# Two half sums for every f32 tile of a fused GNN stage, and a loop over two spans at once

## The reference

```python
for l in range(3):                     # gated network
    m = x @ weight[l]
    agg = segment_sum(m[src] * edge_weight[:, None], dst)
    gi, gh = agg @ w_ih.T + b_ih, x @ w_hh.T + b_hh
    r, zg = sigmoid(i_r + h_r), sigmoid(i_z + h_z)
    x = (1 - zg) * tanh(i_n + r * h_n) + zg * x
...
for W, b in ((W0, b0), (W1, b1), (W2, b2)):
    x = relu((x + segment_sum(x[src], dst)) @ W.T + b)
out = layernorm(x0 + ...)              # after each network
```

## Time and profile before

| What | Value |
|---|---|
| Median of 3 runs | 3116.35 us (3116.19 to 3117.13) |
| Profiled execution, its own time | 3116.43 us |
| Its span, first to last instruction | 3114.7 us |
[...]
| TensorE, VectorE, ScalarE busy | 3055.5 us, 1107.2 us, 909.9 us |
| Packets of TensorE's instruction fetches (q8) | 60, of 16 KB |

### The profile page before, as it was taken

The page is one execution under the profiler, slowest core; times in us unless marked ns, Lnnn a source line. Parts: engine busy times, 40 slices in busy tenths (PEclk is TensorE's granted clock), DMA queues, the critical chain, the costliest instruction groups (busy, mean ns, idle before and its releaser), DMA issues.

```text
span 3114.7 us, 74296 instructions
## 1 busy us (share of the span) xinstructions
PE 3055.5 (98%) x29956; PEld 1975.7 (63%) x29956; DVE 1107.2 (36%) x3061; ACT 909.9 (29%) x2123; POOL 291.1 (9%) x500
## 2 busy tenths in 40 slices
PE   5999999999999999999999999999999999999998
PEld 4788888888888865555555555555555555555554
DVE  5788888888888600000001010111130010001111
ACT  5666666666666510000001010011130010001111
POOL 3222222222222200000000000000000000000000
PEclk9999999999999999999999999999999999999999
DMA  5565555555555587677676777676658777786884
GB/s 183 211 248 246 224 224 246 246 234 224 237 247 240 224 331 273 264 287 279 265 274 251 280 282 282 262 269 272 258 201 332 294 288 280 298 304 260 306 310 164
DMA packets 135446, 809.63 MB, mean 260 GB/s; under 512 B 7972, under 2 KB 17432, under 8 KB 120776
## 3 DMA queue, kind: packets, MB, share of 16 engines
q1 hardware_dynamic: 129704, 800.52, 65.5%
q0 software_dynamic: 4368, 7.97, 0.9%
q10 hardware_dynamic: 1296, 0.01, 0.0%
HBM read 566.04 MB, written 242.44 MB: 260 GB/s over the span
## 4 chain that ended last, share of the span: by engine, by line
PE 98%; issue 1%; DMA 0%; DVE 0%; ACT 0%; POOL 0%; DVEq 0%; POOLq 0%; ACTq 0%
PE ps L758 33%; PE ps L924 25%; PE ps L1003 19%; PE ps L996 11%; PE ps L768 1%; PE ps L769 1%; PE ps L1029 1%; PE ps L746 1%; PE ps L1030 1%; PE ps L771 1%; PE ps L770 1%; PE ps L903 1%; PE ps L1075 0%; PE ps L892 0%; PE ps L1031 0%
## 5 line engine op out<-in xcount | busy, mean ns | idle before, releaser
L758 PE MATMUL ps<-ring,Y 128*128 128x448 f32 x2744 | 1035.7, 539 | 0.0
L758 PEld LDWEIGHTS ps<-ring,Y 128*128 128x128 f32 x2744 | 521.1, 190 | 508.8 <-issue 508.8
L924 PE MATMUL ps<-ring,Y 128*128 128x448 f16 x4116 | 780.6, 352 | 0.0
L1364 ACT ACTIVATE ring<-ps 128x392 f16<-128x392 f32 (+1 forms) x1568 | 654.1, 505 | 303.0 <-PE ps L996 298.0
L924 PEld LDWEIGHTS ps<-ring,Y 128*128 128x128 f16 x4116 | 402.7, 98 | 373.8
L1003 PE MATMUL ps<-ring,Y 128*128 (+1 forms) x2720 | 610.3, 367 | 0.4 <-ACT shared L1326 0.4
L1003 PEld LDWEIGHTS ps<-ring,Y 128*128 128x128 f32 x2720 | 487.1, 190 | 15.5 <-ACT shared L1326 0.8
L996 PEld LDWEIGHTS ps<-shared 64*128 64x128 bf16 x18816 | 337.3, 94 | 129.2 <-ACT ring L1364 82.1
L996 PE MATMUL ps<-shared 64*128 64x49 bf16 (+1 forms) x18816 | 386.7, 190 | 19.3 <-issue 16.3
L1717 DVE TENSOR_TENSOR shared<-shared 128x400 bf16<-128x400 bf16 x1176 | 396.4, 391 | 0.0
L1433 DVE SCALAR_TENSOR_TENSOR shared<-ps,bhh,shared 128x448 f32<-128x448 f32 x28 | 19.1, 684 | 775.4 <-ACT shared L1151 775.4
(11 more groups left out here) (151 smaller groups left out, 1234.7 us busy)
## 6 DMA issues: line engine op xcount, KB each, us to landing
ring<-adj_w SPq DMA_DIRECT2D x84, 2688.0 KB, 8.9
adj_w<-ring SPq DMA_DIRECT2D x56, 2744.0 KB, 12.2
ring<-adj_h SPq DMA_DIRECT2D x42, 2800.0 KB, 9.4
ring<-adj_h SPq DMA_DIRECT2D x42, 2688.0 KB, 9.1
ring<-adj_w SPq DMA_DIRECT2D x28, 2912.0 KB, 9.5
adj_h<-ring SPq DMA_DIRECT2D x56, 1372.0 KB, 5.0
x_keep<-xT SPq DMA_DIRECT2D x1, 3136.0 KB, 10.7
shared<-x_keep SPq DMA_DIRECT2D x1, 3136.0 KB, 15.4
```

The lines of the kernel that those rows point to most:

```text
L758: mm = pe.matmul(ps[:, bank, 0:GW], Y[:, h, :], ring[:, s, :, h - h0, :], start=(h == 0), stop=(last and h == TILES - 1))
L924: mm = pe.matmul(ps[:, par, 0:GW], part[:, h, :], ring_h[:, par, s, :, h - h0, :], start=(h == 0 and part is Y_high), stop=(h == TILES - 1 ...
L1364: act.activation(strip[:, :, c0:c0 + UNIT * WIN].rearrange("p h (d j) -> p d h j", d=WIN), psum_unit(a)[:, :, kind, :, :].rearrange("p d j ...
```

## The change

All 49 f32 tiles of every span are added in halves: rows 0 to 63 into bank 4 and rows 64 to 127 into bank 5. ScalarE copies both sums into two buffers. The gates take both: r, z and the input part of n each become a sum over two terms for the aggregate, so nine matmuls instead of six, of which the first two need only `x` and stand ahead of the wait for the sums. The banks of the coverage check, transpositions and gates move (transpositions now share bank 7 with the gates' n part, and wait for VectorE to have read it). In the tail the gates of span 26 come ahead of the first 13 tiles, and VectorE's addition of the two sums is gone. In TensorE's list the inner loop over slots is written out, so the body of the loop holds two spans and the slot is a constant.

```diff
-        AGG_BANK, COLUMN_BANK, RZ_BANK, IH_BANK = 4, 5, 6, 7
-        HALF_BANK = 0
-        agg_span = aggS[0][:, 0:SPAN]
+        RZ_BANK, IH_BANK, COLUMN_BANK = 6, 7, 7
+        AGG_BANKS = 4, 5
+        ROW_HALVES = [slice(r * P // 2, (r + 1) * P // 2) for r in range(2)]
+        first_banks = 5, 6
+        agg_spans = [a[:, 0:SPAN] for a in aggS]
...
                 for h in range(lo, hi):
-                    mm = pe.matmul(ps[:, AGG_BANK, 0:SPAN], Y[:, h, :],
-                                   strip_w[:, bass.ds(slot, 1), :, h, :].rearrange("p o b c -> p (o b) c"),
-                                   start=(h == 0), stop=(h == TILES - 1))
+                    for rows, bank in zip(ROW_HALVES, AGG_BANKS):
+                        mm = pe.matmul(ps[:, bank, 0:SPAN], Y[rows, h, :], strip_w[rows, slot, :, h, :],
+                                       start=(h == 0), stop=(h == TILES - 1))
...
-                pe.wait_ge(s_fev, START + n + 1)
-                if isinstance(n, int) and n == GATHERS - 1:
-                    pe.wait_ge(s_half, 1)
                 pe.wait_ge(s_frz, START + 2 * n)
                 pe.wait_ge(s_fgv, START + GV * n)
-                for c in range(2):
-                    half = ps[:, RZ_BANK, c * SPAN:(c + 1) * SPAN]
-                    pe.matmul(half, wT[:, c, :], agg_span, start=True, stop=False)
-                    pe.matmul(half, wT[:, 3 + c, :], xg, start=False, stop=True)
-                pe.matmul(ps[:, IH_BANK, 0:SPAN], wT[:, 2, :], agg_span, start=True, stop=True)
-                pe.matmul(ps[:, IH_BANK, SPAN:2 * SPAN], wT[:, 5, :], xg, start=True, stop=True).then_inc(s_fgate, 1)
+                r_z = [ps[:, RZ_BANK, c * SPAN:(c + 1) * SPAN] for c in range(2)]
+                pe.matmul(ps[:, IH_BANK, SPAN:2 * SPAN], wT[:, 5, :], xg, start=True, stop=True)
+                pe.matmul(r_z[0], wT[:, 3, :], xg, start=True, stop=False)
+                pe.wait_ge(s_fev, START + 2 * (n + 1))
+                for a in agg_spans:
+                    pe.matmul(r_z[0], wT[:, 0, :], a, start=False, stop=(a is agg_spans[1]))
+                pe.matmul(r_z[1], wT[:, 4, :], xg, start=True, stop=False)
+                for a in agg_spans:
+                    pe.matmul(r_z[1], wT[:, 1, :], a, start=False, stop=(a is agg_spans[1]))
+                for a in agg_spans:
+                    mm = pe.matmul(ps[:, IH_BANK, 0:SPAN], wT[:, 2, :], a, start=(a is agg_spans[0]),
+                                   stop=(a is agg_spans[1]))
+                mm.then_inc(s_fgate, 1)
...
                     if k == TRANSPOSE_AT:
+                        if n_gates is not None:
+                            pe.wait_ge(s_fgv, START + GV * n_gates + 2)
                         slots_to_partitions(t + 1)
...
                     if k == FIRST_BATCH:
-                        pe.wait_ge(s_fev, t)
+                        pe.wait_ge(s_fev, START + 2 * (t - 1))
...
             with pe.Fori(0, GATHERS // 2 - 1) as i:
-                with pe.Fori(0, 2) as slot:
+                for slot in range(2):
                     build_span(2 * i + slot + 2, slot, 2 * i + slot)
 
-            pe.wait_ge(s_fev, GATHERS)
+            pe.wait_ge(s_cola, GATHERS + 1)
+            fused_gates(GATHERS - 2)
             pe.wait_ge(s_bev, EV * UNITS * (1 + BATCHES * GATHERS))
             add_tiles(0, 0, SH)
-            fused_gates(GATHERS - 2)
-            pe.wait_ge(s_cola, GATHERS + 1)
             pe.wait_ge(s_found, 1)
+            pe.wait_ge(s_fgv, START + GV * (GATHERS - 2) + 2)
             pe.matmul(ps[0:1, COLUMN_BANK, 0:1], covered[:, :], ones[:, :], start=True, stop=True).then_inc(s_cov, 1)
-            add_tiles(0, SH, WHOLE_ROWS)
-            add_halves(0, WHOLE_ROWS, TILES)
+            add_tiles(0, SH, TILES)
...
-                act.activation(by_unit(agg_span), natural(ps[:, AGG_BANK, 0:SPAN]), ACT.Copy).then_inc(s_fev, 1)
+                for agg_span, bank in zip(agg_spans, AGG_BANKS):
+                    act.activation(by_unit(agg_span), natural(ps[:, bank, 0:SPAN]), ACT.Copy).then_inc(s_fev, 1)
...
-            dve.wait_ge(s_fev, START + GATHERS)
-            dve.tensor_tensor(by_unit(agg_span), by_unit(agg_span), natural(ps[:, HALF_BANK, 0:SPAN]), ALU.add)\
-               .then_inc(s_half, 1)
```

More of the change, by code:

```diff
@@ L40 @@
 SH = 13
-WHOLE_ROWS = 37
 HALF_TILES = [(0, 25), (25, 49)]
@@ L291, in gnn_program @@
         s_fagg = sem("s_fagg")
-        s_half = sem("s_half")
         s_fev = sem("s_fev")
@@ L1059, in _ @@
                 for k in range(n):
-                    mm = pe.transpose(ps[:, 6 + j % 2, k * P:(k + 1) * P], Y[:, c + k, :], ident[:, :])
+                    mm = pe.transpose(ps[:, first_banks[j % 2], k * P:(k + 1) * P], Y[:, c + k, :], ident[:, :])
                 mm.then_inc(s_setp, 1)
@@ L1074, in _ @@
                     for h in range(c, c + n):
-                        mm = pe.matmul(ps[:, 6 + k % 2, (h - c) * P:(h - c + 1) * P], xT[:, tile_cols(h)], gw[:, 0, :],
+                        mm = pe.matmul(ps[:, first_banks[k % 2], (h - c) * P:(h - c + 1) * P], xT[:, tile_cols(h)],
+                                       gw[:, 0, :],
                                        start=True, stop=True)
@@ L1343, in evac_span @@
                         act.wait_ge(s_yp0, k + 1)
-                        act.activation(Y[:, c:c + n, :], ps[:, 6 + k % 2, 0:n * P].rearrange("p (c f) -> p c f", f=P), ACT.Copy)\
+                        act.activation(Y[:, c:c + n, :], ps[:, first_banks[k % 2], 0:n * P].rearrange("p (c f) -> p c f", f=P), ACT.Copy)\
                            .then_inc(s_ye0, 1)
@@ L1370, in _ @@
                 act.wait_ge(s_setp, j + 1)
-                act.activation(xT[:, tile_cols(c, n)], ps[:, 6 + j % 2, 0:n * P], ACT.Copy).then_inc(s_xt, 1)
+                act.activation(xT[:, tile_cols(c, n)], ps[:, first_banks[j % 2], 0:n * P], ACT.Copy).then_inc(s_xt, 1)
             act.wait_ge(s_setp, NC + 1)
@@ L1745, in _ @@
                               mybir.AxisListType.XY, ALU.add).then_inc(s_found, 1)
+            fused_mix(GATHERS - 2)
             dve.wait_ge(s_cov, 1)
             dve.tensor_scalar(flag[:, :], ps[0:1, COLUMN_BANK, 0:1], float(N_EDGES), None, ALU.is_equal).then_inc(s_flag, 1)
-            fused_mix(GATHERS - 2)
             fused_blend(GATHERS - 2)
-            dve.wait_ge(s_fev, START + GATHERS)
-            dve.tensor_tensor(by_unit(agg_span), by_unit(agg_span), natural(ps[:, HALF_BANK, 0:SPAN]), ALU.add)\
-               .then_inc(s_half, 1)
             fused_mix(GATHERS - 1)
```

## The result

The changed kernel takes 3306.23 us (median of 4 runs, 3305.37 to 3307.55) against 3116.32 us before in the same session: 1.0609 times the time, interval 1.0591 to 1.0628, 190 us slower. The direction was forecast; the time lies above the range, whose upper end was 3257 us.

The account below looks back on a forecast made before the run. The prediction took TensorE, busy 98% of the span, as the bound. Visits -68 us and gates +32 us gave -36 us, the unrolled loop's fetching +143 us: from 3116.4 us to 3222 us, range 3078 to 3257 us.

Parts of the forecast that it names:

- The whole tiles' visits: TensorE's switches between 64-row builds and 128-row f32 tiles: halves save 0.21 us at each of 324, -68 us (0 to -100).
- The gates: Gate matmuls on TensorE: nine f32 ones instead of six, 0.38 us each, 28 times, +32 us, hidden by nothing.
- Their sum: Visits and gates together, before any cost of unrolling the loop: -36 us.
- The body fetched again in every iteration: TensorE's unrolled loop: the body outgrows the instruction store, all 14.3 blocks fetched anew each iteration, about 190 fetches in all.
- Rival A: The body of two spans stays in the store, no fetches in the loop: 3081 us (3048 to 3149); chance 0.20.
- The price of fetching: TensorE's loop: 9.2 us an iteration for blocks (7.3 to 11.2), 2.3 us a jump; together +143 us (+90 to +175).
- The jump: Jump back in TensorE's loop to code not in the store: 2.3 us each (0 to 2.9), 12 times, 28 us.
- rival D: VectorE becomes the bound if fetches are free, costing at most 1 us a span: 3108 us; counted within Rival A.
- B: The loop's code is fetched again but hidden, only the jump costing: 3109 us; chance 0.06.
- C: The switches give nothing and the store is outrun: 3291 us, or 3148 us with the body resident; chance 0.04.

Follow-up runs that it names:

- the second run: The kernel before with only TensorE's inner loop written out (whole tiles, two spans in the body): 3160.25 us against 3099.4 (1.0196).
- the wide halves: The changed kernel with one span in the body and two neighbouring tiles as one pair of 448-column halves streamed from `Y`: 3082.46 us against 3116.54 (0.989).
- the first run: The changed kernel with TensorE's loop rolled up to one span in the body, halves multiplying `Y` instead of the strips: 3390.66 us against 3099.4 (1.0939).
- The kernel without a loop: The changed kernel with all 26 spans of TensorE's loop written out, no jump left: 3219.85 us against 3099.4 (1.0381).

## Why the prediction was wrong

**The whole tiles' visits, right.** -68 us rested on 0.21 us a batch from the tail's switch of rows and from f16 beside f32. The trace has 1.60 for 1.71 and 0.78 for 0.88. It isn't the register instructions that fell away: whole tiles with the slot a constant still last 1.71 and the builds 0.89 (508.42, 509.31 and 511.02 us in the second run). Shown.

**The gates, right.** +32 us: nine matmuls at 0.38 us, no wait before the sums.

**Their sum, right to 2 us.** -36 us forecast, -34.1 us measured with the wide halves, whose visits and builds last as long as the change's.

**The body fetched again in every iteration, right.** 14.3 blocks forecast, 16 fetches in the iteration shown and 205 more in all (190 forecast). A slip in the count of fetched records (the earlier trace rows give 774 + 775 = 1549 for the first window, not 1559) changes nothing: one fetch per 240 either way. That the store keeps "one of 6.5 blocks and not one of twice the size" was a guess between rows; the runs put its end between 1725 and 1837 instructions, 6.7 to 7.2 blocks of 256. The size of a block shows best where code runs straight on: from 200 to 1000 us there is one fetch of 16 KB for every 257 instructions, 32388 for 126 fetches in the whole tiles without a loop and 34952 for 136 in the halves without one. Rival A's condition was never close: half of the new body is already too large, as the first run shows with 1830 instructions and 149 fetches.

**The price of fetching, wrong: this is the step that failed.** It was "the middle, 9.2" us an iteration for the blocks and "I take 2.3" us for the jump, together +143 us with an upper bound of +175. Measured, against the 3082 us that the change is worth without fetches: 224 us. The kernel without a loop splits them: 155 us for blocks (115 forecast, 141 the bound) and 68 us for jumps (28 forecast, 35 the bound), so each of the two terms was 40 us too small. The stalls were as many as foreseen, five over 1 us in the iteration shown (one of them put down to VectorE), but up to 6.0 us long where 3 was the most foreseen. The price of a block was read from whole tiles, in the loop's first pass, and carried over to halves as if a block cost the same whatever is in it. It doesn't: in code that runs straight on it is 0.34 us a block in whole tiles and 0.87 us in halves. A batch of halves has 128 instructions in 2.38 us and one of whole tiles 112 in 2.60 us, so TensorE reaches the end of a block in 4.8 us instead of 5.9. That this rate is the cause fits the two prices, but was not varied by itself and stays open; the halves' other properties (64 rows, two banks) cost nothing where no fetch is needed. The first pass's own loss, 0.79 us a block, was no good measure of whole tiles either: it is twice what they pay over the whole run. That it lies near the halves' 0.87 is luck.

**The jump.** I bounded it by the longest single stall. In the change it brings two stalls, 2.2 to 3.5 and 3.9 to 6.0 us in the four iterations from 285 to 560 us, and taking all jumps away gives 5.7 us each. In whole tiles with two spans in the body a jump is worth little: 60.9 us with 12 jumps and 52.5 us without, each in its own session, 0.7 us a jump. It isn't the halves that make it dear, though. The whole tiles with 1837 instructions jump back 25 times, pay 256 us, and have 225 fetches more; less 27 us for the added matmuls and 0.34 us a fetch, that leaves 6 us a jump (an estimate). The same sum for the first run, with 34 us for the change, 227 fetches and 0.87 us each, gives 5 us. So three of the four bodies pay 5 to 6 us a jump and the whole tiles of two spans don't; why stays open. Moving the target in its block moved the stalls and didn't cheapen them.

**Idle and slow.** TensorE's waits in the changed kernel from 154 to 1220 us, nearly all of its loop:

```profile
PE ps L996 <- issue: 119.4, 65, 6.0
PE ps L1004 <- issue: 26.8, 17, 2.5
PE ps L996 <- DVE shared L1713: 22.0, 12, 1.9
```

That is 168 us in all, against 5.8 us in the kernel before, and leaves some 60 of the 224 us (5 of them are stalls from 1220 to 1290 us). The granted clock was at half for 140 us of that stretch and never in the kernel before. The gates' matmul above took twice its step there, so work done at half the clock can account for up to 70 us (an estimate, half of the 140); the rest was not taken apart further. Of the 168 us, 22 are put down to VectorE, in one wait an iteration. Each of these waits ends 2.5 to 2.7 us after a fetch has started, where 30 of the 40 stalls over 1 us put down to issue (154 to 1050 us) end after 2.2 to 2.5, so most of the 22 us is likely the fetch's as well. In the wide halves TensorE never waits for VectorE, so it isn't a bound by itself (rival D).

**Rivals A, B and C.** B (hidden fetches) would have left "issue" at 5.4 us; it is 146. What was said for it holds: from 1100 to 3110 us the kernel before has 40 instruction fetches and no wait put down to issue on TensorE's matmuls. It didn't carry over to the fused stage. C (switches that give nothing) fell with the visits and with the 34 us of the wide halves. A (the body stays) fell with the 147 fetches from 200 to 1000 us.

## What to carry to other kernels

Before a loop is unrolled on TensorE, count the instructions of its body (two for a bf16 matmul, four for an f32 one here) and see whether they still fit; here a step from 1725 to 1837 instructions took a kernel from 9 us slower to 256 us slower, where the added matmuls account for some 18 us of the step. Look in the list of DMA queues for instruction packets inside the loop and for "issue" in TensorE's waits: neither is named after a line, and busy shares show little of it (TensorE was 97% busy in the kernel that unrolling alone made 61 us slower). A price of fetching measured on one kind of code needn't hold for another (0.34 and 0.87 us a block here). And a gain that is real (34 us net, with TensorE on 64 rows in builds and tiles alike) was lost here because the code that gets it no longer fitted.

## What the hardware showed that I had not expected

- Between bf16 and f32 matmuls that both read 64 rows, TensorE's next weight load starts with the last matmul (506.97 us both): 1.60 us for 16 half passes and 0.78 us for 48 build matmuls, 0.21 us less for the pair than with tiles on 128 rows.
- A stall for code ends 2.2 to 2.5 us after a fetch has started, in all 44 stalls over 1 us of the kernel without a loop.
- The end of TensorE's instruction store is soft: with 1781 instructions most iterations of one execution fetched nothing and four fetched anew, 36 packets in 800 us and four waits of 4.2 us in the mean (16.9 / 4).
- One span of halves in the body was slower than two: 3391 us against 3288 (an estimate for that session, 1.0609 x 3099.4). Neither fits, and the one has 25 jumps, the other 12; that the jumps make the difference fits their price, but the matmuls' operand differs too.
- VectorE stalled for 5 us once in two spans in the kernels with two weight parts, together with packets of another instruction queue (56 in 800 us); in the same 800 us of the kernel before it has neither.
